# Key attention of layer 0 with 32-row score tiles, steps spread further apart, spreading and part of the sums on GpSimd

## The reference, cut to what matters

```python
q = split_heads(x @ Wq); k = split_heads(x @ Wk); v = split_heads(x @ Wv)
scores = jnp.einsum('bqd,bkd->bkq', q, k) / jnp.sqrt(D)     # D = 128
attn = jax.nn.softmax(scores, axis=-1)                      # over the queries
out = jnp.einsum('bkq,bkv->bqv', attn, v)
z = merge_heads(out) @ Wo
z = _l2_normalize(z) @ Wff
z = gelu(_l2_normalize(z), approximate=False)
```

## Time and profile before

| what | us |
|---|---|
| median of 3 runs (lowest, highest) | 2054.62 (2052.76, 2059.99) |
| the profiled execution, whole | 2049.46 |
| its span, first to last instruction | 2047.5 |
| mean granted TensorE clock | 0.841 of full speed |
| TensorE, VectorE, ScalarE, GpSimd busy | 1486.3, 1260.1, 697.3, 583.2 |

### The profile page before, as it was taken

One profiled execution on the slowest core, in us unless ns is written; L12 is line 12 of the kernel. 1 busy time (PEld: TensorE's weight loads), 2 busy tenths in 40 slices (PEclk: granted clock), 3 DMA queues, 4 the chain that ended last, 5 costly groups with the idle time before them and its releaser, 6 DMA issues. The chain is left out here.

```text
span 2047.5 us, 42138 instructions
## 1 busy us (share of the span) xinstructions
PE 1486.3 (73%) x13310; PEld 1208.9 (59%) x13310; DVE 1260.1 (62%) x3518; ACT 697.3 (34%) x1705; POOL 583.2 (28%) x1089
## 2 busy tenths in 40 slices
PE   6999799997699962039994999961069936557564
PEld 3777478886477751039983999941058725445353
DVE  5888499885888865014442766653011149969896
ACT  2666334332566630012221554420023312223232
POOL 4555210011111021720007554023710067311221
PEclk9999899999799975569996999965579967768578
DMA  4112000000000000137761111000157711000001
GB/s 150 49 49 52 18 1 0 0 0 1 19 23 21 20 4 9 51 107 204 204 174 43 41 36 31 18 1 22 51 146 200 192 42 40 7 24 19 1 1 41
DMA packets 109033, 108.09 MB, mean 53 GB/s; under 512 B 12656, under 2 KB 88432, under 8 KB 108784
## 3 DMA queue, kind: packets, MB, share of 16 engines
q1 hardware_dynamic: 100720, 89.74, 16.1%
q0 software_dynamic: 8192, 16.79, 2.9%
HBM read 81.32 MB, written 25.17 MB: 52 GB/s over the span
## 5 line engine op out<-in xcount | busy, mean ns | idle before, releaser
L2249 DVE COPY e_xT<-e_pX 128x256 f32<-128x256 f32 x72 | 30.6, 424 | 316.8 <-PE e_pX L2310 316.8
L2310 PE MATMUL e_pX<-W,e_rows 128*128 128x128 f32 x144 | 28.7, 282 | 213.8 <-DMA e_rows<-slots_in 212.6
L2321 PE MATMUL e_H<-e_xT,e_w_up 128*128 128x256 f32 x736 | 173.9, 384 | 1.0 <-DMA e_w_up<-in_f_dram 1.0
L2321 PEld LDWEIGHTS e_H<-e_xT,e_w_up 128*128 128x128 f32 x736 | 136.4, 193 | 17.7 <-DVE e_xT L2249 1.4
L2310 PEld LDWEIGHTS e_pX<-W,e_rows 128*128 128x128 f32 x144 | 18.4, 145 | 216.2 <-DMA e_rows<-slots_in 216.0
L2331 PEld LDWEIGHTS e_pY<-e_w_down,e_h 128*128 128x128 f32 x992 | 119.5, 192 | 25.3 <-issue 17.2
L2331 PE MATMUL e_pY<-e_w_down,e_h 128*128 128x128 f32 x992 | 124.8, 277 | 12.4 <-ACT e_h L2298 11.3
L765 PEld LDWEIGHTS f_pZ<-f_Pr,f_vsp 128*128 128x128 f32 x1024 | 119.2, 192 | 3.0 <-issue 1.1
L765 PE MATMUL f_pZ<-f_Pr,f_vsp 128*128 128x64 f32 x1024 | 117.9, 273 | 0.0
L2170 POOL DMA_INDIRECT slots_in<-R,r_put x96 | 92.2, 960 | 57.1 <-issue 28.9
L428 DVE TENSOR_REDUCE a_mx<-a_S 128x8 f32<-128x1024 f32 x64 | 78.1, 1220 | 30.7 <-PE a_S L513 30.5
(11 more groups left out here) (418 smaller groups left out, 4332.5 us busy)
## 6 DMA issues: line engine op xcount, KB each, us to landing
e_w_up<-in_f_dram SPq DMA_DIRECT2D x40, 384.0 KB, 3.6
e_w_down<-in_f_dram SPq DMA_DIRECT2D x32, 322.0 KB, 3.0
e_rows<-slots_in SPq DMA_DIRECT2D x72, 128.0 KB, 2.9
slots_out<-e_y SPq DMA_DIRECT2D x72, 128.0 KB, 3.6
e_w_up<-in_f_dram SPq DMA_DIRECT2D x32, 256.0 KB, 3.7
e_w_down<-in_f_dram SPq DMA_DIRECT2D x40, 192.0 KB, 3.2
slots_in<-Y SPq DMA_DIRECT2D x32, 160.0 KB, 2.5
a_cK<-in_ctxT_dram SPq DMA_DIRECT2D x64, 64.0 KB, 1.8
```

What stands on the lines that cost most here:

```text
L2321: i = nc.tensor.matmul(H[:, banks * p + b, CHUNK * c:CHUNK * (c + 1)], up[:, p, at:at + P], xT[:, p, :], start=True, stop=True)
```

## The change

The stage is rebuilt with other tiles, another split between the engines and other lags.

- Projections: three matmuls over both sequences at once (q, k, v), all into `pA`, and one eviction by ScalarE into a ring `qkv` of eight tiles. x's transpose now goes to the free quarter of the same bank, and waits until the tile before it is evicted.
- Scores: the 16 heads are taken as four groups of four (32 channels). `spread` repeats q four times, made by GpSimd in one operation for the tile. For each half, four matmuls with 32-row, 64-column weights and 256 columns give the scores of two sequences and two groups. Each half has one buffer of scores, not two.
- The exponentials lie in a ring of six tiles; GpSimd adds their halves and then quarters (`add_up`), VectorE adds the last 16 of each.
- The product with V uses 32 matmuls with 64-row, 32-column weights from a padded `V`.
- Output: one matmul. Squares and the copy to `Y` are both ScalarE's.
- Lags: the exponential moves to 6, `add_up` is at 7, the division moves from 6 to 8, the product from 7 to 9, the eviction of z to 10, output and squares to 11; `take_xt` stays last in ScalarE's list. All lists are straight.
- One memset (V, 1280 elements a partition) takes the place of three (`blk` 512, `vsp` 4352, `zT` 512). VectorE's first copies wait for it. Two packed weights of 256 columns become 128.

```diff
-    RUN = P + 8
+    SG, HG, RING, DEPTH = 4, 4, 8, 6
...
-        blk = sb("blk", [P, 2, 2, P])
-        spread = sb("spread", [P, 2, 2, GH, T])
-        Pr = sb("Pr", [P, 2, HEADS, T])
+        qkv = sb("qkv", [P, RING, 3, P])
+        spread = sb("spread", [P, 2, 2, HG, T])
+        Pr = sb("Pr", [P, DEPTH, HEADS, T])
         mx = sb("mx", [P, 2, HEADS])
+        part2 = sb("part2", [P, 2, HEADS, 32])
+        part4 = sb("part4", [P, 2, HEADS, 16])
...
-        vsp = sb("vsp", [P, 2, 2, GH * RUN])
...
+        V = sb("V", [P, 2, SG, 160])
...
-        vraw = net.R
-        S = ps("S", [P, 2, 1024])
-        pX, pA, pZ, pY = [ps(n, [P, 512]) for n in ("pX", "pA", "pZ", "pY")]
+        S = ps("S", [P, 2, 2, 512])
+        pA = ps("pA", [P, 512])
+        pZ = ps("pZ", [P, 2, 512])
+        pY = ps("pY", [P, 512])
...
         @block.gpsimd
         def _(pool):
             ln.setup(pool)
-            for t in (blk, vsp, zT):
-                nc.gpsimd.memset(t[:], 0.0).then_inc(s_zero, 1)
-            pipeline(pool, NT, [(1, lambda u, p: ln.pool_rstd(pool, u, p))])
+            nc.gpsimd.memset(V[:], 0.0).then_inc(s_zero, 1)
+            mask = w("mask4").unsqueeze(1).unsqueeze(3).broadcast_to([P, 2, HG, T])
+
+            def spread_q(u, p):
+                done(pool, s_qkv, u)
+                free(pool, s_S, u, per=2)
+                src = qkv[:, u % RING, 0].rearrange("p (b t) -> p b t", b=2).unsqueeze(2)
+                nc.gpsimd.tensor_tensor(spread[:, p], src.broadcast_to([P, 2, HG, T]), mask, ALU.mult
+                                        ).then_inc(s_spread, 1)
+
+            def add_up(u, p):
+                done(pool, s_exp, u)
+                free(pool, s_quart, u)
+                nc.gpsimd.tensor_tensor(part2[:, p], Pr[:, u % DEPTH, :, 0:32], Pr[:, u % DEPTH, :, 32:64], ALU.add
+                                        ).then_inc(s_half, 1)
+                done(pool, s_half, u)
+                free(pool, s_sum, u)
+                nc.gpsimd.tensor_tensor(part4[:, p], part2[:, p, :, 0:16], part2[:, p, :, 16:32], ALU.add
+                                        ).then_inc(s_quart, 1)
+
+            pipeline(pool, NT, [(7, add_up), (1, lambda u, p: ln.pool_rstd(pool, u, p)), (4, spread_q)],
+                     straight=True)
...
         def _(dve):
...
-            def take_spread(u, p):
-                done(dve, s_v, u)
-                free(dve, s_S, u, per=2)
-                for g in range(2):
-                    src = pA[:, 384 + T * g:384 + T * g + T].unsqueeze(1).broadcast_to([P, GH, T])
-                    i = nc.vector.tensor_tensor(spread[:, p, g], src, mask, ALU.mult)
...
-            def softmax(g):
+            def softmax(half):
                 def fn(u, p):
...
+                    Sg = S[:, half, :, 0:256].rearrange("p r (h k) -> p r h k", k=T)
+                    top = mx[:, p].rearrange("p (r u h) -> p r u h", r=2, u=2)[:, :, half]
+                    out = Pr[:, u % DEPTH].rearrange("p (r u h) k -> p r u h k", r=2, u=2)[:, :, half]
+                    dve.wait_ge(s_S, 2 * u + half + 1)
+                    nc.vector.tensor_reduce(top, Sg, AX, ALU.max).then_inc(s_mx, 1)
+                    dve.wait_ge(s_mx, 2 * u + half + 1)
+                    free(dve, s_z, u, bufs=DEPTH)
+                    free(dve, s_half, u, bufs=DEPTH)
+                    nc.vector.tensor_tensor(out, Sg, top.unsqueeze(3).broadcast_to([P, 2, HG, T]),
                                             ALU.subtract).then_inc(s_sub, 1)
                 return fn
 
             def divide_v(u, p):
-                done(dve, s_exp, u)
-                nc.vector.tensor_reduce(sums[:, p, :], Pr[:, p], AX, ALU.add).then_inc(s_sum, 1)
+                done(dve, s_quart, u)
+                free(dve, s_rd, u)
+                nc.vector.tensor_reduce(sums[:, p, :], part4[:, p], AX, ALU.add).then_inc(s_sum, 1)
...
+                nc.vector.reciprocal(rden[:, p, :, 0], sums[:, p, :]).then_inc(s_rd, 1)
                 done(dve, s_rd, u)
                 free(dve, s_z, u)
-                for b in range(2):
-                    r = slice(64 * b, 64 * b + 64)
-                    out = vsp[r, p].rearrange("p g (h x) -> p g h x", x=RUN)[:, :, :, 64 * b:64 * b + 8]
-                    i = nc.vector.tensor_tensor(
-                        out, vraw[r, u, :].rearrange("p (g h c) -> p g h c", g=2, c=8),
-                        rden[r, p].broadcast_to([64, 2, GH, 8]), ALU.mult)
-                i.then_inc(s_vs, 1)
-
-            def keep_w(u, p):
-                done(dve, s_y, u)
-                nc.vector.tensor_copy(net.Y[:, u, :], pY[:, 128:256]).then_inc(s_w, 1)
-
...
+                dst = V[:, p].rearrange("p g (h c) -> p g h c", c=40)[:, :, :, 0:8]
+                nc.vector.tensor_tensor(dst, qkv[:, u % RING, 2].rearrange("p (g h c) -> p g h c", g=SG, h=HG),
+                                        rden[:, p].rearrange("p (g h) c -> p g h c", g=SG).broadcast_to([P, SG, HG, 8]),
+                                        ALU.mult).then_inc(s_vs, 1)
...
+            dve.wait_ge(s_zero, 1)
...
-            pipeline(dve, NT, [(4, take_spread), (9, keep_w),
-                               (2, lambda u, p: ln.vector_apply(dve, u, p)),
-                               (0, lambda u, p: ln.vector_stats(dve, u, p)),
-                               (1, lambda u, p: ln.vector_moments(dve, u, p)), (6, divide_v),
-                               (5, softmax(0)), (5, softmax(1))])
+            nc.vector.tensor_copy(wow[:, D:2 * D], pA[:, 0:D]).then_inc(s_wzs, 1)
+            nc.vector.tensor_copy(wow[:, 0:D], w("f0_wo")).then_inc(s_wzs, 1)
+            pipeline(dve, NT, [(2, lambda u, p: ln.vector_apply(dve, u, p)), (5, softmax(0)), (5, softmax(1)),
+                               (1, lambda u, p: ln.vector_moments(dve, u, p)),
+                               (0, lambda u, p: ln.vector_stats(dve, u, p)), (8, divide_v)], straight=True)
...
             def take_xt(u, p):
                 done(act, s_xt, u)
...
-                nc.scalar.activation(xT[:, p, :], pX[:, 0:128], ACT.Copy).then_inc(s_xts, 1)
-
-            def take_blk(u, p):
+                nc.scalar.activation(xT[:, p, :], pA[:, 384:512], ACT.Copy).then_inc(s_xts, 1)
+
+            def take_qkv(u, p):
                 done(act, s_proj, u)
-                free(act, s_S, u, per=2)
-                for b in range(2):
...
+                free(act, s_S, u, bufs=RING, per=2)
+                free(act, s_vs, u, bufs=RING)
+                nc.scalar.activation(qkv[:, u % RING].rearrange("p a t -> p (a t)"), pA[:, 0:384], ACT.Copy
+                                     ).then_inc(s_qkv, 1)
...
             def exps(u, p):
                 done(act, s_sub, u, per=2)
-                nc.scalar.activation(Pr[:, p], Pr[:, p], ACT.Exp, scale=SCALE).then_inc(s_exp, 1)
+                nc.scalar.activation(Pr[:, u % DEPTH], Pr[:, u % DEPTH], ACT.Exp, scale=SCALE).then_inc(s_exp, 1)
...
             def take_z(u, p):
                 done(act, s_z, u)
                 free(act, s_y, u)
...
+                nc.scalar.activation(zT[:, p].rearrange("p (b t) -> p b t", b=2), pZ[:, :, 0:T], ACT.Copy
+                                     ).then_inc(s_zt, 1)
...
-            pipeline(act, NT, [(9, squares), (7, take_z), (3, take_blk), (5, exps), (2, take_xt)])
+                done(act, s_y, u)
+                nc.scalar.activation(junk[:, :], pY[:, 0:D], ACT.Square,
+                                     accum_out=net.norms[:, 0, u:u + 1]).then_inc(s_sq, 1)
+                nc.scalar.activation(net.Y[:, u, :], pY[:, D:2 * D], ACT.Copy).then_inc(s_sq, 1)
+
+            pipeline(act, NT, [(10, take_z), (6, exps), (3, take_qkv), (11, squares), (2, take_xt)],
+                     straight=True)
...
             def transpose_x(u, p):
                 done(pe, ln.s_xn, u)
                 free(pe, s_xts, u, bufs=1)
-                nc.tensor.transpose(pX[:, 0:128], xn[:, p, :], w("ident")).then_inc(s_xt, 1)
+                free(pe, s_qkv, u, bufs=1)
+                nc.tensor.transpose(pA[:, 384:512], xn[:, p, :], w("ident")).then_inc(s_xt, 1)
 
             def project(u, p):
                 done(pe, s_xts, u)
-                free(pe, s_spread, u, bufs=1)
-                nc.tensor.matmul(pA[:, 128:256], xT[:, p, :], w("f0_wv"), start=True, stop=True)
-                for b in range(2):
...
-                                         xT[:, p, r], start=True, stop=True)
-                        i = nc.tensor.matmul(pA[r, 384 + T * g:384 + T * g + T], w("f0_wq")[:, c],
...
+                free(pe, s_qkv, u, bufs=1)
+                nc.tensor.matmul(pA[:, 0:128], w("f0_wq"), xT[:, p, :], start=True, stop=True)
+                nc.tensor.matmul(pA[:, 128:256], w("f0_wk"), xT[:, p, :], start=True, stop=True)
+                nc.tensor.matmul(pA[:, 256:384], xT[:, p, :], w("f0_wv"), start=True, stop=True
+                                 ).then_inc(s_proj, 1)
+
+            def scores(half):
```

(79 more changed lines are left out.)

52 lines of the change are left out of this document (7 added, 45 removed), and 2 rows, old and new, of the table PACK.

## The result

The changed kernel takes 2068.41 us (median of 6 runs, 2063.51 to 2070.38) where before took 2055.84 (2051.29 to 2060.28). The ratio is 1.0062, 95% interval 1.0043 to 1.0081: slower by 0.6%, where 2030 was forecast, 1.2% faster. The range, 1998 to 2058, missed it. The profiled execution took 2070.4 us with a span of 2068.6.

The account below looks back on a forecast made before the run. Not engine work but the order of dependencies bounds the changed stage: 252.7 + 28 x 7.0 + 3 x 4.6 + 12.5 = 475.0 against 499.8 us. 2054.6 - 24.8 gives 2029.8, say 2030; range 1998 to 2058.

Parts of the forecast that it names:

- the ring: Layer 0 key attention: scores, softmax, moments, rstd, spread, next tile's scores wait on each other; 6.2 us a step at 2.4 GHz.
- Start and end: Key attention's edges: first maximum at 252.7 us; 12.5 us from the last maximum's start to the stage's end.
- the last three periods: Final tiles of the stage, where TensorE's and VectorE's work alone counts: 4.6 us each.
- the clock of the ring: TensorE in key attention: granted clock 0.75, so its 2.3 us become 3.05 and the period 7.0 us; chance 0.43.
- the 28 gated periods: Key attention's steps from the first maximum on, gated by moments, at 7.0 us each.
- the late stage: Old profile, 1963.7 to 1970.5 us: TensorE busy 4.19 of 6.8 us at clock 0.75, taken as model for the new stage.
- The product with V: TensorE in key attention: 64 records at 28 ns, 1.8 us a step, bounds below 0.5 and 3.8, hidden behind the scores.
- the slower rival: Clock stays at 1.2 GHz in key attention: period 8.5 us, time 2085; chance 0.14 together with a lesser form near 2060.
- The page's rule: Skill page warns only of TensorE idle stretches over 2.1 us; by it clock holds: period 6.2, time 2007, chance 0.27.

Follow-up runs that it names:

- the run one step later: Changed kernel with GpSimd's spread first, normalisation behind both softmax halves, x's transpose and all that follows shifted by one step: 1968.66 us, ratio 0.9557.

## Why the prediction was wrong

**Right: the ring.** The order of dependencies held, and so did the claim that no engine would be the bound. The length at 2.4 GHz was forecast as 6.2 and measured as 6.18 in the run with four added matmuls, but that agreement is partly luck: TensorE's part took 2.62 us (forecast 2.3), and the part from the second half's maximum to the next scores 3.56 (1.4 + 1.15 + 1.2 + 0.2 = 3.95). Spread took 1.14 us at the median (forecast 1.2), the scores two by two in rows and columns 1.13 us for eight records at 1.2 GHz and 0.66 at 2.4, the sums lay beside the ring, the normalisation met GpSimd and took 1.06 us without entering the ring. Start and end were near as well: the first maximum at 254.05 (forecast 252.7), the last three periods together 13.7 us (13.8, though as 5.72, 4.0 and 4.0 and not three of 4.6), the end 13.7 us after the last maximum's start (12.5).

**Wrong: the clock of the ring.** The step that failed is "at clock 0.75 TensorE's 2.3 us in the ring become 3.05". The clock was 0.54, TensorE's part of the ring took 4.69 us, and the 28 gated periods took 225.2 us and not 196. That is 29 of the 31.6 us by which the stage ended later than forecast. Two things led there.

First, 0.75 is a mean over the stretch of the late stage, and was used as if it held for TensorE's work. The same stretch in two halves reads

```profile
1963.70:1967.10 3.40, 0.79 (x7) 0.79 (x8) 3.25 (x14) 0.69 (x3) 1.16 (x2) 1.00 0.00 0
1967.10:1970.50 3.40, 3.40 (x15) 2.93 (x14) 3.22 (x14) 1.33 (x4) 0.89 (x2) 0.50 0.02 5
```

The clock was 1.00 while TensorE had 0.79 us of work and 0.50 while it had 3.40: the late stage did 3.40 of its 4.19 us of work at 1.2 GHz. With 3.40 of each 4.19 at half speed, TensorE's 2.3 us in the ring become about 4.2 and the period 8.1 (an estimate from these rows), much nearer to the 8.26 measured than 7.0.

Second, the rival was struck out with a wrong term. The product with V was put at 1.8 us at 2.4 GHz, from 28 ns a record in tiles of 32 columns over all rows. Tiles of 64 rows by 32 columns took 0.86 us for 64 records at 2.4 GHz and 1.18 at 1.2 GHz; the working had named less than 0.5 as the lower bound and taken 1.8. That cost lies off the ring and did not matter for a step's length at a given clock. But the slower rival was held unlikely because at 1.2 GHz TensorE would be busy almost without a gap, 8.2 us of 8.5. It was busy about 6.1 of 8.26 (73.85 of 100 us), and the clock was 0.50 to 0.63 in the stretches of 40 us from 260 to 460. The reason itself, that without a gap the clock would be full, does not hold for this work either: the run one step later, without added matmuls, was busy for 40.00 of 40 us at 0.50.

**The rival that came true.** Its period of 8.5 was 8.26, with 4.69 + 3.57 us against its 4.6 + 3.95. Its time of 2085 was 17 too high, and even that is closer than its parts: it had the stage end at 530.3 and the end was 506.6. Of these 23.7 us, 12.8 lie in the first 28 periods (8.04 at the mean) and 10.9 in the last three, which it put at 8.2 each; there the clock had risen (0.84 from 480 to 500 us). The kernel as a whole lost about 6 us more than its changed stage, and that made up for a part.

**What the added matmuls do not show.** The run with two of them comes near the forecast's 0.75, 7.0 and 2030. It does not show that a product of 1.8 us would have done the same, since what was added used full tiles and the product does not.

**The page's rule.** The Trainium skill ("TensorE: Matmul & The Clock Gate", "Why this matters for your kernels") warns of idle stretches longer than the 2.1 us of the forecast; by it the clock would hold. The runs do not bear that out. With two added matmuls TensorE's longest idle piece from 300 to 450 us was 1.72 us, and the clock still fell in every second or third step (periods of 6.18 and 7.81); with spread first and none added the longest from 300 to 400 us was 0.86 us, at a clock of 0.81.

## What to carry to other kernels

Where each engine runs a fixed list, cost the rings through the lists before the work of the engines: follow the softmax of one tile over every instruction queued ahead of what the next tile's scores wait for. Here that ring, at 1.2 GHz, made all savings of work worthless, and the order of three entries in one list was worth 82 us. Check an order for rings again after each move; the second one appeared where a step was moved to save 0.7 us.

A change that takes work from TensorE can take its clock too, and a cost that is off the path can still carry the clock. A mean clock over a stretch is not the clock of the work in it: split the stretch where the engine goes from idle to busy and read each part. The busy share alone did not tell the clock here, so cost the path at 1.2 GHz as a case of its own, and test it with added matmuls whose result is not used.

## What the runs showed of the hardware

- Added matmuls that compute nothing made the kernel 39 us faster: busy 73.85 of 100 us at a clock of 0.54, 80.36 at 0.81, 86.30 at 1.00.
- The granted clock does not follow the busy share: 74.87 of 100 us busy at 0.90 in one run, 40.00 of 40 us at 0.50 in another. In the late stage of the kernel before it was 1.00 while TensorE was nearly idle (0.79 of 3.40 us) and 0.50 while it worked (3.40 of 3.40).
- 64 matmul records on tiles of 64 rows by 32 columns, two row groups and four column groups by turns, took 0.86 us at 2.4 GHz and 1.18 us at 1.2 GHz, 13 and 18 ns each. At half the clock the same instructions took only 1.4 times as long.
- VectorE's normalisation of a 128x128 tile took 1.06 us at the median beside GpSimd's spread (1.14 us) and 0.34 where GpSimd was idle.
